# A four-layer convolution kernel, first layer: the first gelu in operations of 4096 columns, the second in place in PSUM, its products added from PSUM in halves, with the statistics between them

## What is computed

```python
y = gelu(x[..., :, None] * w1)                       # 4 values of y for each channel
z = gelu(einsum('bhwim,moi->bhwmo', y, wg))          # 4 projections of 32x32
out = einsum('bhwmc,cm->bhwc', z, w2)
...
x = x + L0(gn(x)); x = x + L1(gn(x)); x = x + L2(gn(x)); x = x + L3(gn(x))
```

## Time and profile before

| | us |
|---|---|
| runs (3): median, lowest, highest | 1149.85, 1148.54, 1150.21 |
| the profiled execution: span, first to last instruction | 1148.0 |
| PE busy with matmuls | 952.7 (83% of the span) |
| DVE busy | 867.1 (76%) |
| ACT busy | 693.3 (60%) |
| POOL busy | 317.6 (28%) |

### The profile page before, as it was taken

How to read it: one execution, slowest core, us unless ns; L and a number is a source line. 1 busy time by engine, 2 the same in 40 slices (tenths; PEclk the granted TensorE clock), 3 DMA queues, 4 the chain that set the end, 5 groups by cost and what they waited for, 6 DMA issues and landing times. The chain is left out here.

```text
span 1148.0 us, 22784 instructions
## 1 busy us (share of the span) xinstructions
PE 952.7 (83%) x6876; PEld 650.8 (57%) x6876; DVE 867.1 (76%) x1211; ACT 693.3 (60%) x860; POOL 317.6 (28%) x265
## 2 busy tenths in 40 slices
PE   5699977979989977845999949799999788676774
PEld 4333327968878875334433349688778683233332
DVE  7477788877757944876687878877769646799796
ACT  5799972323358853547999923234388563366564
POOL 0000009400026720510000066000077403466565
PEclk9799998989989988987999979989999898899897
DMA  9100000000000010233000000000000200024334
GB/s 294 37 0 0 0 0 1 0 1 1 0 1 1 0 73 5 69 114 107 0 0 0 0 1 1 1 1 0 1 1 0 74 0 1 0 86 135 106 114 146
DMA packets 51301, 39.32 MB, mean 34 GB/s; under 512 B 1600, under 2 KB 50880, under 8 KB 51008
## 3 DMA queue, kind: packets, MB, share of 16 engines
q1 hardware_dynamic: 51264, 38.85, 10.7%
HBM read 22.07 MB, written 16.78 MB: 34 GB/s over the span
## 5 line engine op out<-in xcount | busy, mean ns | idle before, releaser
L337 PE MATMUL ps<-work,cst 128*128 128x512 f32 x512 | 237.0, 610 | 17.5 <-ACT work L557 13.7
L337 PEld LDWEIGHTS ps<-work,cst 128*128 128x128 f32 x512 | 94.5, 193 | 158.8 <-issue 144.4
L256 PE MATMUL ps<-ST,work 128*128 x256 | 131.1, 635 | 9.7 <-DVE work L897 7.1
L557 ACT ACTIVATE work<-X,l0s 128x2048 f32 x64 | 136.6, 2140 | 2.6 <-SPq L294 2.6
L564 ACT ACTIVATE work<-ps 128x2048 f32<-128x2048 f32 x64 | 123.1, 1923 | 8.2 <-PE ps L337 8.0
L1019 POOL TENSOR_TENSOR work<-cst,ksum 128x512 f32<-128x512 f32 x64 | 66.2, 1055 | 203.2 <-SPq L294 174.4
L806 DVE TENSOR_TENSOR work<-ps,cst 64x512 f32<-64x512 f32 x128 | 88.2, 689 | 39.1 <-PE ps L404 37.3
L984 POOL TENSOR_TENSOR co<-mv,cst 128x1 f32<-128x1 f32 x8 | 1.5, 191 | 392.1 <-DVEq L246 302.4
L450 PE MATMUL ps<-work,cst 128*64 128x128 f32 x1024 | 103.6, 287 | 6.7 <-ACT work L621 6.7
L586 ACT ACTIVATE work<-ps 128x512 f32<-128x512 f32 x80 | 47.8, 598 | 100.5 <-PE ps L357 100.5
L450 PEld LDWEIGHTS ps<-work,cst 128*64 128x64 f32 x1024 | 88.4, 141 | 18.7 <-issue 9.9
(11 more groups left out here) (99 smaller groups left out, 1774.3 us busy)
## 6 DMA issues: line engine op xcount, KB each, us to landing
work<-x SPq DMA_DIRECT2D x32, 512.0 KB, 4.9
out<-work SPq DMA_DIRECT2D x64, 256.0 KB, 2.8
work<-choose SPq DMA_DIRECT2D x2, 2048.0 KB, 8.4
cst<-consts SPq DMA_DIRECT2D x1, 1009.5 KB, 9.6
cst<-consts SPq DMA_DIRECT2D x1, 64.0 KB, 2.0
```

Of the source, the lines that this page charges most:

```text
L256: return nc.tensor.matmul(ps[:, bank, :], sel[:, n, :], ST[:, ds(s * (4 * H), 4 * H)], start=True, stop=True)
L337: last = pe.matmul(ps[:, 4 * (m % 2) + b, :], wg[:, m, :], yb[:, m, b * BANK:(b + 1) * BANK], start=True, stop=True)
L557: act.activation(yb[:, m, :], X[:, ds(s * PIX + i * CHUNK, CHUNK)], ACT.Gelu, scale=l0s[:, m:m + 1], bias=l0s[:, MULTI + m:MULTI + m + 1]) ...
```

## The change

The unit of y becomes 4096 columns (LONG): one y feeds two halves v = 0 and 1 of 2048 columns. A y and its two halves are called a **pair** here, numbered e from 0 to 15 in a set (4 stretches of columns times 4 multiples). yb now has 3 buffers of 4096 columns. z writes its result over its own input in PSUM, and zb is gone. Each product is split into two halves of 1024 columns that read PSUM. acc holds 4096 columns. A half of PSUM is now freed by the products: the first two banks by the first, the other two by the second. ACT's queue holds, for each pair e: z of (e, 0), then y of e + 2, then z of (e, 1). The 4 bn_stats of half 0 are put between the products of the two halves of the last multiple, those of half 1 between the products of the next stretch's first pair. The loops over s in PE, ACT and DVE, and the loops of stage 1, are written out in Python.

```diff
+LONG = 2 * CHUNK
+PARTS = PIX // LONG
+Y_RING = 3
...
-        work = sb("work", MW + 7168)
+        work = sb("work", 4 * LONG)
...
-        yb, _e = part(0, [DEEP, CHUNK])
-        zb, _e = part(_e, [RING, CHUNK])
-        acc, _ = part(_e, [CHUNK])
+        yb, _e = part(0, [Y_RING, LONG])
+        acc, _ = part(_e, [RING, RING, CHUNK // RING])
...
-        s_zs = rsem("z_ready", "act")
-        s_x1 = rsem("z_added", "dve")
+        s_zs = sem("z_ready")
+        s_x1 = sem("z_half_added")
...
-            with pe.Fori(0, NS) as s:
+            for s in range(NS):
...
-                with pe.Fori(0, PIX // CHUNK) as i:
-                    for m in range(MULTI):
-                        k = s * UNITS + i * MULTI + m
-                        pe.wait_ge(s_y, k + 1)
-                        pe.wait_ge(s_zs, slot(k))
+                for e in range(PARTS * MULTI):
+                    m = e % MULTI
+                    pe.wait_ge(s_y, s * PARTS * MULTI + e + 1)
+                    for v in range(RING):
+                        k = (s * PARTS * MULTI + e) * RING + v
                         for b in range(4):
-                            last = pe.matmul(ps[:, 4 * (m % 2) + b, :], wg[:, m, :], yb[:, m, b * BANK:(b + 1) * BANK],
+                            if b % 2 == 0 and k >= RING:
+                                pe.wait_ge(s_x1, 2 * (k - RING) + 1 + b // 2)
+                            at = v * CHUNK + b * BANK
+                            last = pe.matmul(ps[:, 4 * v + b, :], wg[:, m, :], yb[:, e % Y_RING, at:at + BANK],
                                              start=True, stop=True)
                         last.then_inc(s_zp, 1)
...
-                def gelu_y(i, m):
-                    act.activation(yb[:, m, :], X[:, ds(s * PIX + i * CHUNK, CHUNK)], ACT.Gelu,
+                def gelu_y(e):
+                    nn, m = s * PARTS * MULTI + e, e % MULTI
+                    if nn >= Y_RING:
+                        act.wait_ge(s_zp, RING * (nn - Y_RING) + RING)
+                    at = s * PIX + e // MULTI * LONG
+                    act.activation(yb[:, e % Y_RING, :], X[:, at:at + LONG], ACT.Gelu,
                                    scale=l0s[:, m:m + 1], bias=l0s[:, MULTI + m:MULTI + m + 1]).then_inc(s_y, 1)
 
-                def gelu_z(i, m):
-                    k = s * UNITS + i * MULTI + m
-                    act.wait_ge(s_zp, k + 1)
-                    act.wait_ge(s_x1, slot(k))
-                    act.activation(zb[:, m % 2, :], ps[:, 4 * (m % 2):4 * (m % 2) + 4, :].rearrange("p a b -> p (a b)"),
-                                   ACT.Gelu).then_inc(s_zs, 1)
-
-                gelu_y(0, 0)
-                gelu_y(0, 1)
-                with act.Fori(0, PIX // CHUNK - 1) as i:
-                    for m in range(MULTI):
-                        gelu_y(i + (m + 2) // MULTI, (m + 2) % MULTI)
-                        gelu_z(i, m)
-                for m in range(MULTI):
-                    if m + 2 < MULTI:
-                        gelu_y(PIX // CHUNK - 1, m + 2)
-                    gelu_z(PIX // CHUNK - 1, m)
+                def gelu_z(e, v):
+                    act.wait_ge(s_zp, (s * PARTS * MULTI + e) * RING + v + 1)
+                    z = ps[:, 4 * v:4 * v + 4, :].rearrange("p a b -> p (a b)")
+                    act.activation(z, z, ACT.Gelu).then_inc(s_zs, 1)
+
+                gelu_y(0)
+                gelu_y(1)
+                for e in range(PARTS * MULTI):
+                    gelu_z(e, 0)
+                    if e + 2 < PARTS * MULTI:
+                        gelu_y(e + 2)
+                    gelu_z(e, 1)
...
-                with dve.Fori(0, PIX // CHUNK) as i:
-                    x_in = X[:, ds(s * PIX + i * CHUNK, CHUNK)]
-                    for m in range(MULTI):
-                        k = s * UNITS + i * MULTI + m
-
-                        dve.wait_ge(s_zs, after(k))
-                        dve.wait_ge(s_x1, slot(k) + 1)
-                        dve.scalar_tensor_tensor(acc if m < MULTI - 1 else x_in, zb[:, m % 2, :],
-                                                 c("w2")[:, m:m + 1], acc if m else x_in, ALU.mult, ALU.add
-                                                 ).then_inc(s_x1, 1)
-                    dve.wait_ge(s_x1, after(k))
-                    alone(dve)
+                def measure_x1(e, v):
                     for b in range(4):
-                        dve.bn_stats(stats[:, ds(i * 24 + 6 * b, 6)], X[:, ds(s * PIX + i * CHUNK + b * BANK, BANK)])
+                        bank = e // MULTI * 8 + 4 * v + b
+                        dve.wait_ge(s_x1, 2 * ((s * PARTS * MULTI + e) * RING + v) + b // 2 + 1)
+                        at = s * PIX + bank * BANK
+                        dve.bn_stats(stats[:, 6 * bank:6 * bank + 6], X[:, at:at + BANK])
+
+                for e in range(PARTS * MULTI):
+                    m = e % MULTI
+                    for v in range(RING):
+                        k = (s * PARTS * MULTI + e) * RING + v
+                        dve.wait_ge(s_zs, k + 1)
+                        for hf in range(2):
+                            if m:
+                                dve.wait_ge(s_x1, 2 * (k - RING) + hf + 1)
+                            at = s * PIX + e // MULTI * LONG + v * CHUNK + hf * (CHUNK // 2)
+                            x_in = X[:, at:at + CHUNK // 2]
+                            z = ps[:, 4 * v + 2 * hf:4 * v + 2 * hf + 2, :].rearrange("p a b -> p (a b)")
+                            dve.scalar_tensor_tensor(acc[:, v, hf, :] if m < MULTI - 1 else x_in, z,
+                                                     c("w2")[:, m:m + 1], acc[:, v, hf, :] if m else x_in,
+                                                     ALU.mult, ALU.add).then_inc(s_x1, 1)
+                        if v == 0 and m == MULTI - 1:
+                            measure_x1(e, 0)
+                        if v == 0 and m == 0 and e:
+                            measure_x1(e - 1, 1)
+                measure_x1(PARTS * MULTI - 1, 1)
```

More of the change, by code:

```diff
@@ L543, in _ @@
             act.sem_inc(s_out[1], 64)
-            with act.Fori(0, NS) as s:
+            for s in range(NS):
                 with act.Fori(0, 4) as i:
@@ L695, in _ @@
             start_rings(dve, "dve")
-            with dve.Fori(0, NS) as s:
+            for s in range(NS):
                 def measure(i, u):
```

## The result

| | before | after |
|---|---|---|
| median of 4 runs | 1150.03 us | 1154.58 us |
| lowest to highest | 1148.54 to 1150.23 | 1153.76 to 1156.01 |
| span of the profiled execution | 1148.0 | 1152.0 |

The ratio is 1.004 with a 95% interval of 1.0025 to 1.0054: slower by 4.6 us.

The account below looks back on a forecast made before the run. The prediction took a ring through ACT, DVE and PE, from PSUM release to release, to bound stage 1: +23.4 us for two sets, less 1 for written-out loops, is +22.4 on 1149.85, so 1172.3 us; range 1160 to 1186.

Parts of the forecast that it names:

- Durations: Stage 1 operations: y of 4096 columns 3.86 us, z in place 1.92, product half from PSUM 1.27.
- The ring: Stage 1: PSUM release through product, two projections, z, y and z takes 15.99 us for two pairs, 8.00 per pair.
- The sum for stage 1: Per set: start +1.7 us, 14 pairs +7.1, end +2.9, together 11.7; for two sets 23.4.
- The written-out loops: All stages: less register work in the queues gains 1 us, at most up to 6 more.
- The rival with falls of the clock in stage 1: Stage 1: PE's pauses of about 1.9 us, 7 a set, lower its granted clock; 1209 us, chance 6%.
- The rival in which ACT is the bound: Stage 1: PSUM halves free early enough; 1139 us with z at its lower bound, 3%; 1150 with z as today, 3%.
- the one in which PSUM takes turns: Stage 1: reading and writing one bank alternate, z takes 3.6 us, a pair 10.7; 1255 us, chance 4%.

Follow-up runs that it names:

- the kernel with zb: The changed kernel with z back in SBUF, PSUM freed by z, y still 4096 columns with two buffers, queued behind both z: 1137.74 us.
- The run with the later release: The changed kernel with PE waiting for the second product half, not the first, before the first bank of a PSUM half: 1174.32 us.

## Why the prediction was wrong

Step by step:

- **Durations.** y, z in place, the product half out of PSUM: said 3.86, 1.92 and 1.27 us, measured 3.79, 1.86 and 1.28. That z in place is no dearer than z to SBUF holds: in the kernel with zb it takes 1.87 us. What the Trainium skill says (ScalarE: Activation LUTs, "Step-by-step: what each stage is for"), that ACT writes PSUM faster than SBUF, agrees in sign with these two numbers, by 0.01 us. But their ranges overlap (1.83 to 1.87 and 1.85 to 1.88 us), and two z in a row take 3.64 us in place and 3.62 or more to SBUF, so no run here shows a gain from it.
- **The ring.** Said 15.99 us for two pairs, measured 15.87, with ACT waiting for PE and PE for the product where they were put. The run with the later release confirms it as the bound (17.06 us where 17.1 was said), and with zb, which takes the product out of the ring, stage 1 is back at 133.9 and 134.5 us.
- **The sum for stage 1.** Said +11.7 per set. Measured from the first y: first z after 9.57 us instead of 8.46, +1.1 (said +1.7; up to the first z PE was busy 0.6 us less, 5.7 instead of 6.3, at a granted clock of 0.59 instead of 0.57; with the later release it was 6.7 at 0.53, so this is the clock's luck and not the edit's); the 14 pairs from 51.33 to 162.47 111.1 us instead of 104.8, +6.3 (said +7.1); from there to the last product's end 16.4 instead of 13.9, +2.5 (said +2.9). The stage as a whole: +9.5 and +10.2. Against the written-out kernel with the old stage 1 it is +9.2 and +9.5.
- **The written-out loops: the step that failed.** The prediction took 1 us, as a chosen value, "since the queue works ahead of its engine wherever the engine is busy", and bounded it by some 6. It is 11.8 us, by the run with that edit alone. Two things were missed. The jump back from set 0 to set 1 leaves DVE standing for 3.91 us and makes PE some 3 us late beside it; the "issue" wait of DVE at 502.40 was in the trace of before and was not looked up. And DVE's register work is on the path in stage 2 in spite of 65 busy us in 73.5, because its instructions there are short (0.37 to 0.45 us) and wait for each other. I bounded the gain from the one line with the longest register work, in stage 7, and not from the stages with the most instructions.
- **The clock.** The rival with falls of the clock in stage 1 did not come about: 1.00 from the first z on, over pauses of 1.50 us. But stages 6 and 7 of the second set ran at a higher clock than before, worth some 3 us. The prediction had no term for that.

In sum: +19.7 us in stage 1 less 12 to 13 for the loops elsewhere less 3 for the clock gives the 4 us of the spans. The rival in which ACT is the bound was wrong, as was the one in which PSUM takes turns. The range failed because the term for the loops was bounded too narrowly. With 11.8 us in place of 1 the forecast would have been 1161.5 us; of the 7 us that are left, 3.7 are the two stages 1 (19.7 for 23.4) and 3 the clock, both on the same side.

The kernel with all loops of PE, ACT and DVE written out and stage 1 as before beats both, at 1125.6 us.

## What to carry to other kernels

When a buffer is to be freed by a later engine, add up the ring from release to release, with all that stands in each engine's queue between: here 15.9 us for two pairs against 15.0 of the fullest engine's old work, though no engine was full. A diff that also writes a hardware loop out needs a term of its own, looked up at the jump (the "issue" wait at its end) and in the stages with the shortest instructions, where register work shows in the distance between starts and not in idle time. A table load inside a loop body runs with each pass; here that cost nothing that showed.

## What the runs showed of the hardware

- A jump back of a long hardware loop: 3.91 us in which DVE did nothing. With DVE's loop written out PE's first matmul came 3.9 us after DVE's first instruction, with PE's written out too 0.84: PE was some 3 us late. A jump of DVE's inner loop in stage 2: 0.47 us, 0.3 with the outer loop written out.
- Register instructions ahead of short DVE instructions: 0.42 us per strip of 16 instructions, seen as no idle time; with DVE's inner loops written out as well as the outer ones 9.2 us less.
- ACT reads and writes the same 4 banks of PSUM in one operation at full rate: 1.86 us for 2048 columns, against 1.87 from PSUM to SBUF. Neither its own traffic nor DVE's reads slowed it.
- PE's granted clock stayed at 1.00 over pauses of 1.50 us, one in every 15.9 us, and over 1.71 and 1.09 us by turns, two in every 17.1 us, with the later release.
- The same instructions of stages 5 to 7 took 87.3 us at granted clocks of 0.90, 0.83 and 0.94 in the three stages, and 91.2 us at 0.86, 0.68 and 0.89.
